# Rewriting the head of an adaLN, selective-scan and mixture-of-experts kernel, and GpSimd's form of the state scaling

## The reference

```
mod = (silu(c) @ wmod).reshape(4, 6, 1, 128)       # sa, ca, ga, sb, cb, gb
h = layernorm(x) * (1 + ca) + sa                   # x: 4 x 1024 x 128
gate = sigmoid(h @ W2 + b2)
u = sigmoid(causal_conv4(h @ W1 + b1) + conv_b)    # 256 channels
xp = u @ x_proj_w                                  # 64 + 16 + 16 columns
delta = softplus(xp[:64] @ dt_proj_w + dt_proj_b)
B, C = xp[64:80], xp[80:96];  A = -exp(A_log)      # 16 states per channel
state[n] = exp(delta * A[n]) * state[n] + delta * B[n] * u
y = sum_n state[n] * C[n] + u * D_skip
x = x + ga * ((y * gate) @ Wo + bo)
h = layernorm(x) * (1 + cb) + sb
x = x + gb * moe(h)                                # 8 experts of 352, the best 2 of each token
```

## Time and profile before

| | |
|---|---|
| median of 3 runs | 698.61 us (697.56 to 700.04) |
| profiled execution, its own time | 697.62 us |
| its span in the profile | 695.8 us |
| PE busy | 615.6 us (88%) |
| DVE busy | 552.0 us (79%) |
| ACT busy | 535.4 us (77%) |
| POOL busy | 517.3 us (74%) |

### The profile page before, as it was taken

One profiled execution on the slowest core, in us unless ns is written; L12 is line 12 of the kernel. 1 busy time (PEld: TensorE's weight loads), 2 busy tenths in 40 slices (PEclk: granted clock), 3 DMA queues, 4 the chain that ended last, 5 costly groups with the idle time before them and its releaser, 6 DMA issues.

```text
span 695.8 us, 14462 instructions
## 1 busy us (share of the span) xinstructions
PE 615.6 (88%) x4435; PEld 512.3 (74%) x4435; DVE 552.0 (79%) x1170; ACT 535.4 (77%) x1000; POOL 517.3 (74%) x453
## 2 busy tenths in 40 slices
PE   3986889989988998997999898769789999999995
PEld 3444757867767675785777677658578999999994
DVE  4347779999989999999999999989986586555554
ACT  3268998997998997999799799797834756566650
POOL 3147969988799899989989999986964647644441
PEclk9999999999999999999999999899999999999998
DMA  7030336434943454534455335466711223222545
GB/s 237 0 123 2 102 86 161 135 93 129 320 122 106 115 129 128 162 101 109 119 148 136 105 100 129 128 182 178 177 30 55 65 62 86 81 69 65 152 145 193
DMA packets 65194, 82.92 MB, mean 119 GB/s; under 512 B 6960, under 2 KB 55152, under 8 KB 61024
## 3 DMA queue, kind: packets, MB, share of 16 engines
q1 hardware_dynamic: 59648, 70.78, 37.2%
q0 software_dynamic: 4320, 9.12, 4.0%
q10 hardware_dynamic: 1152, 2.10, 0.8%
HBM read 52.19 MB, written 29.78 MB: 118 GB/s over the span
## 4 chain that ended last, share of the span: by engine, by line
PE 43%; ACT 36%; DVE 11%; issue 7%; DMA 1%; POOL 1%; DVEq 0%; SPq 0%; ACTq 0%; POOLq 0%
PE psum L589 26%; PE psum L593 16%; ACT S L1006 12%; ACT dA L1014 11%; DVE ring L1370 5%; ACT L953 1%; ACT xn L918 1%; ACT soft L946 1%; ACT soft L945 1%; ACT soft L953 1%; ACT soft L950 1%; ACT L1014 1%; DMA ring<-results 1%; ACT hT L900 1%; ACT psum L958 1%
## 5 line engine op out<-in xcount | busy, mean ns | idle before, releaser
L559 POOL TENSOR_TENSOR ring<-ring,Cb 128x1024 f32<-128x1024 f32 x128 | 279.6, 2186 | 36.7 <-DVE ring L1370 36.2
L593 PEld LDWEIGHTS psum<-ident,S 128*128 128x128 f32 x1024 | 118.6, 143 | 113.5 <-issue 67.7
L593 PE MATMUL psum<-ident,S 128*128 128x128 f32 x1024 | 159.2, 279 | 42.7 <-DVE ring L1370 14.3
L1014 ACT ACTIVATE dA<-delta,A 128x512 f32<-128x512 f32 x256 | 178.6, 716 | 10.3 <-DVE ring L1370 10.1
L1006 ACT ACTIVATE S<-duT,BT 128x256 f32<-128x256 f32 x384 | 166.4, 501 | 24.3 <-DVE duT L1110 20.2
L593 PE MATMUL psum<-ident,ring 128*128 128x128 f32 x1088 | 159.5, 278 | 4.2 <-DMA ring<-results 3.8
L1370 DVE TENSOR_TENSOR_SCAN ring<-dA,state,psum 128x512 f32<-128x512 f32 x128 | 157.6, 1265 | 1.0 <-PE psum L593 0.4
L1370 DVE TENSOR_TENSOR_SCAN ring<-dA,psum 128x512 f32<-128x512 f32 x128 | 150.2, 1206 | 8.8 <-PE psum L593 8.2
L593 PEld LDWEIGHTS psum<-ident,ring 128*128 128x128 f32 x1088 | 129.5, 144 | 5.2 <-DMA ring<-results 4.3
L581 POOL DMA_INDIRECT results<-xn,result_at x71 | 68.7, 968 | 74.6 <-DVE xn L1503 64.9
L589 PE MATMUL psum<-uT,S 128*128 128x128 f32 x852 | 107.2, 275 | 1.0 <-DVE uT L1481 1.0
(11 more groups left out here) (218 smaller groups left out, 734.2 us busy)
## 6 DMA issues: line engine op xcount, KB each, us to landing
Cb<-c_rows SPq DMA_DIRECT2D x32, 1024.0 KB, 6.0
token_rows<-zeros SPq DMA_DIRECT2D x64, 272.0 KB, 7.1
uT<-token_rows SPq DMA_DIRECT2D x71, 68.0 KB, 1.8
ring<-results SPq DMA_DIRECT2D x8, 512.0 KB, 5.0
xT<-in_xT SPq DMA_DIRECT2D x4, 512.0 KB, 4.9
out_T<-xT ACTq DMA_DIRECT2D x8, 256.0 KB, 2.8
stage<-in_xT SPq DMA_DIRECT2D x6, 256.0 KB, 7.7
gateup_w<-in_gate SPq DMA_DIRECT2D x1, 1408.0 KB, 9.5
```

Source lines behind the costliest of these rows:

```text
L559: nc.gpsimd.tensor_tensor(ring[:, k % RING, :, 0:BANK], ring[:, k % RING, :, 1:], Cb[:, group_ % 2, own, :].unsqueeze(1).to_broadcast([P, ...
L593: return nc.tensor.matmul(out, block_in, ident[at, at], is_transpose=True, start=start, stop=True, skip_group_check=True)
L1014: nc.scalar.activation(dA[:, (k * HALVES + a) % DA_SLOTS, :], delta[:, s % 2, a, :], ACT.Exp, scale=A[:, a, n:n + 1]).then_inc(da_ready, 1)
```

## The change

The head (everything ahead of the step loop) is no longer two windows of gaps but a list of its own on each engine.

- Roots: blocks 0 and 1 get theirs from GpSimd too, one `pow` each (`front_root`), VectorE adding epsilon before and multiplying by the mean after (`front_shift`, `front_means`); the Ln, Exp and Newton steps go. Blocks 2 and 3, 4 and 5 follow in the head, 6 and 7 in the first scan segment (GpSimd gap 1, VectorE gap 6). The tail's root has its epsilon added on VectorE in gap 18.
- Folding W1 with the conv weights is done by GpSimd in two halves (`fold`).
- Banks: `home(name, f)` gives the results of blocks 0 and 1 banks of their own (`HEAD_HOMES`), and block 1's h its own tile.
- Orders: see the lists. ScalarE makes both halves of the first softplus in a row with one load of the Ln table; VectorE's part is `first_softplus`, which keeps its intermediate in SBUF (`yg`). TensorE does the first xproj product before the transposes of u. The statistics of the last two blocks stand right ahead of the first scan.
- Idle products: `warm(8)` ahead of the modulation product and `warm(6)` after the first raw transposes, into bank 3, read by nobody.
- One-tensor scaling: GpSimd makes each of its chunks of S with one TENSOR_SCALAR, with BT's column as the per-partition scalar and a second operation times 1.0. `add_bias` gets the second operation as well.
- `minus_half` stands elsewhere in memory, `eps` is gone and `frs` smaller.

```diff
@@ constants @@
 def pool_scaled(k):
-    return sum(pool_chunks(j) > 0 for j in range(k + 1))
+    return sum(pool_chunks(j) for j in range(k + 1))
...
+        HEAD_HOMES = {("xn", 1): "B4", ("u0", 1): "B1", ("u1", 0): "FT", ("u1", 1): "FT", ("uT0", 0): "FT", ("uT1", 0): "B0",
+                      ("gate0", 0): "B0", ("gate1", 0): "B4", ("dt1", 0): "FA", ("dT1", 0): "FA", ("bt", 0): "B1"}
+        def home(name, f):
+            return HEAD_HOMES.get((name, f), "FB" if name in ("xproj", "bt", "dt0", "dt1", "dT0", "dT1") else "FA")
@@ gpsimd @@
+            def front_root(first, last, shifts):
+                part = slice(CS * first, CS * last)
+                pool.wait_ge(fshift_ready, shifts)
+                nc.gpsimd.tensor_tensor(frs[:, 0, part], frs[:, 0, part], minus_half[:, part], ALU.pow).then_inc(froot_ready, 1)
+            def fold(a):
+                at = slice(a * P, (a + 1) * P)
+                nc.gpsimd.tensor_tensor(w1c[:, :, at], w1[:, at].unsqueeze(1).to_broadcast([P, CONVK, P]),
+                                        convb.rearrange("p (d k) -> p k d", k=CONVK)[:, :, at], ALU.mult).then_inc(w1c_ready, 1)
...
-                    nc.gpsimd.tensor_tensor(S[:, k % S_SLOTS, CS - own:, :], duT[:, s % 2, CS - own:, :],
-                                            BT[:, s % 2, CS - own:, n:n + 1].to_broadcast([P, own, MLP]), ALU.mult
-                                            ).then_inc(scaled_pool, 1)
+                    for c in range(CS - own, CS):
+                        nc.gpsimd.tensor_scalar(S[:, k % S_SLOTS, c, :], duT[:, s % 2, c, :], BT[:, s % 2, c, n:n + 1], 1.0,
+                                                ALU.mult, ALU.mult).then_inc(scaled_pool, 1)
+            front_root(0, 1, 1)
+            pool.wait_ge(loaded["attn"], 16 * ATTN_LOADS)
+            fold(0)
+            front_root(1, 2, 2)
+            fold(1)
             pool.wait_ge(mod_step, MOD_STEPS)
-            for window in (-2, -1):
-                for gap in range(GAPS):
-                    gap_work(gap, window)
+            add_bias(0)
+            for b in (1, 2):
+                front_root(b * SEG, (b + 1) * SEG, b + 2)
+                add_bias(b)
+            add_bias(BATCH - 1)
@@ tensor @@
+            def warm(count):
+                for _ in range(count):
+                    product(bank(3)[:, 0:P], mean_w[:, :], mean_w[:, :])
+            pe.wait_ge(mod_step, 1)
+            warm(WARM_FIRST)
...
             for f in range(SEG):
                 raw_turns(f)
+            warm(WARM_SECOND)
+            front(14, 0)
             pe.wait_ge(corr_ready, HALVES)
...
+            pe.wait_ge(w1c_ready, 1)
+            for k in range(CONVK):
+                tap(0, 0, k)
             pe.wait_ge(mod_step, MOD_STEPS)
+            front(14, 1)
+            for f in (SEG, SEG + 1):
+                raw_turns(f)
+            pe.wait_ge(w1c_ready, HALVES)
+            for k in range(CONVK):
+                tap(0, 1, k)
             for a in range(HALVES):
-                product(FT[:, a * P:(a + 1) * P], ones[:, :], Ddiag[:, a, :])
+                pe.wait_ge(read[f"u{a}"], 1)
+                pe.wait_ge(const_ready, XBIAS)
+                last = product(FB[0:PROJ, :], xproj[:, a, :], u[:, 0, a, :], a == 0, a == HALVES - 1)
+            last.then_inc(filled["xproj"], 1)
+            last_read["FB"] = (read["xproj"], 1)
+            for f in (SEG + 2, SEG + 3):
+                raw_turns(f)
+            project(3, 0)
+            last_read["FB"] = (delta_ready, 1)
+            project(6, 0)
+            last_read["FA"] = (delta_ready, HALVES)
+            project(9, 0)
+            front(30, 0)
+            front(1, 0)
...
+            for f in (SEG + 4, SEG + 5):
+                raw_turns(f)
+            front(2, 0)
+            pe.wait_ge(const_ready, CONSTS)
+            for k in range(CONVK):
+                tap(1, 0, k)
+            front(5, 0)
+            project(24, 0)
+            tap(1, 1, 0)
+            project(26, 0)
+            pe.wait_ge(read["u0"], 2)
+            front(30, 1)
+            pe.wait_ge(stat_read, CS * SEGS)
             for a in range(HALVES):
                 turn_in(0, a)
+            tap(1, 1, 1)
+            pe.wait_ge(read["gate1"], 1)
+            for a in range(HALVES):
+                turn_in(1, a)
+                tap(1, 1, 2 + a)
+            front(31, 1)
@@ scalar @@
-            act.wait_ge(mod_step, 2)
-            for step in range(2):
-                front_seeds(step)
+            front(13, 0)
+            act.wait_ge(mod_step, MOD_STEPS)
+            act.wait_ge(zeroed, 2)
+            front(16, 0)
             act.wait_ge(loaded["attn"], 16 * ATTN_LOADS)
             nc.scalar.activation(A[:, :, :], A[:, :, :], ACT.Exp).then_inc(a_exp, 1)
...
+            front(13, 1)
+            act.wait_ge(const_ready, ZHALF)
+            front(22, 0)
+            front(16, 1)
+            front(28, 0)
+            act.wait_ge(const_ready, XBIAS)
+            front(2, 0)
+            for gap in (5, 8, 9, 10):
+                project(gap, 0)
+            for a in range(HALVES):
+                one_more(0, a)
+            bt_copy(0)
+            for a in range(HALVES):
+                nc.scalar.activation(lw[:, a, :], ev[:, a, :], ACT.Ln, bias=1.0).then_inc(lw_ready, 1)
+            front(22, 1)
+            act.wait_ge(const_ready, A_SIGNED)
+            for a in range(HALVES):
+                decay(0, a)
+            scale_in(0)
+            act.wait_ge(const_ready, B2HALF)
+            front(7, 0)
+            scale_in(1)
+            for a in range(HALVES):
+                decay(1, a)
+            front(4, 0)
+            front(28, 1)
@@ vector @@
             for f in range(SEG):
                 raw_stats(f)
+                front_shift(f, f + 1)
+            front_means(0, 1, 1)
...
+            for b in (1, 2):
+                for f in (b * SEG, b * SEG + 1):
+                    raw_stats(f)
+                front_shift(b * SEG, (b + 1) * SEG)
+                if b == 2:
+                    front(31, 0)
+                    front(2, 0)
+                    dve.wait_ge(drow_filled, 1)
+                    V.tensor_copy(Drow[:, :], bank(4)[:, 0:MLP]).then_inc(const_ready, 1)
+                front_means(b * SEG, (b + 1) * SEG, b + 2)
             dve.wait_ge(const_ready, CONSTS)
...
+            first_softplus()
+            for gap in (25, 27):
+                project(gap, 0)
+            for f in (SEGS - 2, SEGS - 1):
+                raw_stats(f)
+            front_shift(SEGS - 2, SEGS)
+            front(31, 1)
```

More of the change, by code:

```diff
@@ L222, in stat_bank @@
         def stat_bank(f):
[L224 to L231, removed]
+            return bank(f if f < SEG else 2 + f % 2)
         PX = bank(6)[:, 0:P]
@@ L718, in gap_work @@
                 call = routed(window)
-                if window == -1 and 14 <= gap < 27:
-                    front_ = None
                 if tail_ is not None:
@@ L757, in start_y, with raw_turns @@
                                          start=(c == c0 and a == 0), stop=True, skip_group_check=True)
+            def warm(count):
+                for _ in range(count):
+                    product(bank(3)[:, 0:P], mean_w[:, :], mean_w[:, :])
+            def raw_turns(f):
+                pe.wait_ge(loaded_x[f // SEG], 16)
+                wait(pe, stat_read, CS * (f - 1) if f >= SEG + 2 else 0)
+                for c in range(CS):
+                    last = turn(stat_bank(f)[:, c * P:(c + 1) * P], xT[:, f * BANK + c * P:f * BANK + (c + 1) * P])
+                last.then_inc(stat_filled, 1)
+            pe.wait_ge(mod_step, 1)
+            warm(WARM_FIRST)
             pe.wait_ge(loaded["c"], 48)
@@ L764, in _ @@
             pe.wait_ge(setup, SETUP)
-            def raw_turns(f):
-                pe.wait_ge(loaded_x[f // SEG], 16)
-                if f == SEG + 2:
-                    pe.wait_ge(mod_step, MOD_STEPS)
-                wait(pe, stat_read, CS * (f - 2) if f >= SEG + 3 else 0)
-                for c in range(CS):
-                    last = turn(stat_bank(f)[:, c * P:(c + 1) * P], xT[:, f * BANK + c * P:f * BANK + (c + 1) * P])
-                last.then_inc(stat_filled, 1)
             for f in range(SEG):
                 raw_turns(f)
+            warm(WARM_SECOND)
+            front(14, 0)
             pe.wait_ge(corr_ready, HALVES)
@@ new lines, in _ @@
+            project(6, 0)
[3 more added lines that the diff above has]
+            front(1, 0)
+            pe.wait_ge(const_ready, D_MADE)
+            pe.wait_ge(read["xn"], 2)
+            for a in range(HALVES):
+                last = product(bank(4)[:, a * P:(a + 1) * P], ones[:, :], Ddiag[:, a, :])
+            last.then_inc(drow_filled, 1)
+            for f in (SEG + 4, SEG + 5):
+                raw_turns(f)
+            front(2, 0)
@@ L937, in project @@
                 if gap == 12:
[L938 to L940 removed]
+                    bt_copy(f)
+                if gap in (12, 21):
```

(5 more changed lines are left out.)

262 lines of the change are left out of this document (117 added, 145 removed).

## The result

The changed kernel takes 694.11 us (693.12 to 695.04, 5 runs) against 698.41 (697.40 to 700.04, 5 runs): ratio 0.994, 95% interval 0.9923 to 0.9958. It gained 4.3 us where 13.7 were forecast, and lies 4.1 us above the end of the range. Its profiled execution has 694.11 us of its own and a span of 692.1, 3.7 less than the span before.

What follows compares the result with a forecast made beforehand. ScalarE was taken to set the pace from the end of the head on, so head savings of 8.65 + 5.0 = 13.65 us come off the end. From 697.6 that left 683.9, for the median 684.9; range 683 to 687.

Steps and rivals of the forecast that it cites:

- Step 1: Head, statistics to first tap: ScalarE starts 3.9 us earlier; first tap at 15.2 us with the clock high.
- Step 2: Head, folded weights moved from VectorE to GpSimd: 1.05 to 2.1 us a half, no effect on the time.
- Step 3: Head, TensorE's clock: with idle products high at the first tap, 2.95 us less for the first passes.
- the first rival: Head: the clock is low at the taps, 10.0 us gained, 688.5 us; chance 0.22.
- Steps 4 to 7: Head, second half of u to ScalarE's loop: 1.3, 6.7 and 0.95 us less, then 2.65 more.
- X: The point in the head where the projection is complete, forecast at 26.0 us, before at 34.67.
- Step 8: Scan phase: shorter GpSimd scaling, the last root and the tail's shift on VectorE change nothing in the time.
- The slower side: Scan phase: GpSimd's single-tensor scaling costs 0.89 us instead of 0.62, giving 707 us; chance 0.04.
- The freed GpSimd time: Scan phase: TensorE gets its scaling sooner, half a microsecond a segment, giving 681 us; chance 0.13.
- The missed-wait rival: Head: the hand-made order has an overlooked wait, 3 to 6 us more, 689.5 us; chance 0.13.

Runs made afterwards that it cites:

- roots_first: shift_back with GpSimd making both early roots ahead of both folds: 686.61 us.
- shift_back: The kernel after with the tail's epsilon added on GpSimd again, as before: 688.46 us.
- scaling_alone: The kernel before with the new one-tensor scaling on GpSimd and nothing else: 696.75 us, ratio 0.9990.
- more_idle_products: roots_first with 12 instead of 6 idle products behind the first raw transposes: 685.31 us.
- scaling_back: The kernel after with GpSimd's scaling again as one product with the broadcast column of BT: 698.96 us.
- shift_alone: The kernel before with the tail's epsilon added by VectorE in gap 18 and nothing else: 707.02 us.
- no_idle_products: roots_first with no idle products at all: 687.01 us.

## Why the prediction failed, step by step

**Step 1, statistics to first tap.** The first tap came at 16.36, not at 15.2. The arithmetic of what was removed holds: the root of GpSimd took 1.05 us from 10.51 (estimate 1.04 from 10.4). Missing is the 1.4 us of the held product, a term that the step doesn't have: "Nothing else is waited for". roots_first, which takes away what held it, has the product in 0.16.

**Step 2, the fold.** 1.53 us a half, between the bounds, there at 13.08 and 15.54 and waited for by no tap. "I take nothing" was still wrong: it looked at who waits for the fold, not at whom the fold holds: VectorE's product with the means lasts 1.49 us beside the first half and 1.48 beside the second, and 0.16 in roots_first beside none.

**Step 3, the clock.** 5.14 us for the first passes, 1.7 over the forecast, whose 2.95 us are the difference of 6.39 and 3.44 in the earlier trace rows, the lengths of the same eight passes that the low and the high clock stand for here; no run shows a frequency. It is not one execution's chance: the five profiles with the head and the idle products of the kernel after have 5.14 to 5.96. The forecast took one unbroken stretch of work to be enough, and named the low clock as the first rival; the kernel fell between, with the low clock for part of the passes (5.14 between 3.44 and 6.39). The table of windows has the granted clock at 0.50 in 16 to 18 us, 0.67 in the next and 1.00 behind it:

```profile
12.00:14.00 2.00, 0.27 (x2) 0.00 (x0) 1.75 (x6) 0.87 (x3) 2.00 (x2) 1.00 1.01 391
...
16.00:18.00 2.00, 1.64 (x2) 0.84 (x3) 1.58 (x7) 1.97 (x4) 0.65 (x1) 0.50 0.04 15
18.00:20.00 2.00, 2.00 (x4) 0.85 (x3) 0.51 (x4) 1.16 (x4) 0.00 (x0) 0.67 0.01 4
20.00:22.00 2.00, 2.00 (x8) 0.93 (x7) 0.00 (x0) 0.09 (x1) 0.00 (x0) 1.00 0.00 0
```

TensorE was busy for 0.27 of the 2 us from 12 to 14, while the transposes waited for the normalised rows, which waited for the held product.

**Steps 4 to 7** held to a few tenths. From the end of the first passes to X: 28.91 - 21.50 = 7.41, 8.68 before: 1.27 less, forecast 1.3. Deltas at X + 10.1 and X + 11.4 (forecast 10.5 and 11.9), first scaling at 42.74 = X + 13.83 (13.85), first scan at X + 16.58 (17.0), ScalarE's step 2 at X + 20.82 (21.0), with the 1.93 us of ScalarE waiting before the second tanh of block 1 that was named. The head is short of the forecast by 13.65 - 10.92 = 2.7 us: 1.16 from step 1, 1.70 from step 3, little else.

**Step 8 failed**, the step with no sum in it: "In the tail a shift of four columns goes from GpSimd (0.19) to VectorE: nothing." It costs 5.2 us by shift_back, in the profiles 1.0 us a segment (58.95 against 57.95). Its price was taken from the row of the same instruction on the other engine, and VectorE was thought to have slack for 0.2 us a segment. It has hardly any for 1.5: it is busy 55.15 of 59 us, and the scans behind it feed everyone. GpSimd's wait for the scans over 172 to 404 us was 11.1 us; between the third and the sixth load of Ln it is 7.0 before, 14.8 after and 10.7 in shift_back. The other terms of step 8 held: scaling 0.48 us (taken 0.40, bounds 0.40 and 0.89), the last root 1.64 (1.7), and no segment time from a shorter scaling beyond the 1 us of scaling_alone.

Of the 10.0 us by which the span misses the sum (13.65 forecast, 3.7 measured), the head has 2.7, the scans 5.7 and the experts 1.5.

**The rivals.** The slower side, a scaling of 0.89 us, did not come. The freed GpSimd time is the 1.2 us above, not 3. The missed-wait rival put the fault in the order of the roots in the head and came to 689.5; the waits were as planned, and no semaphore is at fault. A held engine has no releaser in the profile: it shows as a busy row that is too long, as the 1.82 us at 249.38, which names none.

**What stays open.** The experts took 1.5 us more of the span. In the nine profiles with the new head that stage has 185.0 to 187.0 us, in the three with the old one 183.0 to 184.6. In seven of the nine the last gather of results stands in the chain with 7.3 to 7.9 us; with the old head it has 5.8 to 6.0. The piece of the kernel after:

```profile
679.59 7.27 DMA ring<-results
```

The nine also share the other placement in memory (`minus_half`, `eps`, `frs`), so that is as good a suspect as the head; neither was tried alone, nor a further run of the old head.

The best version is more_idle_products, 685.31 us and 0.9818 (0.9781 to 0.9855), but roots_first and its other variants are not told apart from it; all of them beat both kernels. That they come near the forecast of 684.9 is in part luck: in all of them GpSimd's fold still holds the second product with the means, the experts take 1.5 us or more longer than before, and the first passes are at the high clock in some and not in others.

## What to carry to other kernels

Price an instruction that changes engines by its neighbours there: in this kernel a TENSOR_SCALAR of four columns from SBUF to SBUF on VectorE lasted, in six of its eight times, until the end of what GpSimd was running, up to 2.54 us in the kernel after and 2.8 in scaling_back and shift_alone; a column at a time it took 0.32 for the four, on GpSimd itself 0.2. In a profile look for rows whose mean is far above their minimum and which end together with a row of GpSimd (here a mean of 1.46 us and a minimum of 0.16): no wait and no releaser is shown for the row at 249.38. When one edit looks good beside another, run the square of both before crediting either: here the new scaling was worth 4.5 us beside the fault and 1.2 without it.

## What the runs showed that was not expected

*Which forms are held.* By GpSimd's products of two tensors: TENSOR_SCALAR with one source of four columns (up to 2.54 us), and instructions with two SBUF inputs, even of one column (1.09 us in the kernel before, 1.48 to 1.58 in the kernel after). By its one-tensor instructions with two operations too: the two-input row at 15.67 above (0.99 us), and a TENSOR_SCALAR of two columns that in roots_first ended with GpSimd's add_bias (14.72, 1.12 us):

```profile
14.87 1.00 DVE L1526 TENSOR_SCALAR zhalf<-zhalf 128x2 f32<-128x2 f32 x1
```

Not held: one source and one column (0.144 us), and the RECIPROCAL (0.18 us). Beside the add_bias of the kernel before, which has one operation and ran from 12.33 to 15.27, VectorE's instructions with two SBUF inputs took 0.17 us (14.76 and 14.96); beside that of the kernel after the product with the means took 0.17 at 27.06, begun 0.05 us behind it, and was held at 34.23 (0.42 us). Nor did GpSimd's power hold one-source instructions that started in it, from 13.04 to 14.05 in the kernel after:

```profile
13.29 0.25 DVE L1517 TENSOR_SCALAR xproj<-xproj 128x192 f32<-128x192 f32 x1
...
13.60 0.16 DVE L1519 TENSOR_SCALAR gaquarter<-mod 128x4 f32<-128x4 f32 x1
```

Why these differ is open; each was seen only where this kernel happens to put it.

*The fold's pattern* on GpSimd costs 1.53 us for 512 elements, against 1.05 for the scaling product of 512 in the earlier trace rows.

*The clock at the start isn't the program's alone.* Up to the modulation the kernel after and roots_first issue the same work to TensorE, the eight idle products with it. The same twelve products of the modulation took, in the one and in the other:

```profile
5.21 2.69 PE L596 MATMUL psum<-siluc,ring 128*128 128x4 f32 x12 [0.31 <-ACT siluc L1071]
```

```profile
5.28 1.47 PE L598 MATMUL psum<-siluc,ring 128*128 128x4 f32 x12 [0.45 <-ACT siluc L1073]
```

So a forecast of the level at a given microsecond of the head has an uncertainty, here 1.2 us for twelve products, that the eight idle products don't take away. The column of the granted clock doesn't help there: it reads 1.00 over 16 to 22 us of no_idle_products, while the eight passes take 5.93 us, near the 6.39 of the low clock. The window and TensorE's timeline:

```profile
16.00:22.00 6.00, 6.00 (x13) 2.45 (x12) 2.00 (x8) 2.45 (x7) 0.98 (x1) 1.00 0.02 6
```

```profile
15.48 5.93 PE L598 MATMUL psum<-hT,w1c 128*128 128x512 f32 x8
```

In the kernel before the column reads 1.00 too from 20 to 26 us, in the passes that took 6.39 us:

```profile
20.00:26.00 6.00, 6.00 (x9) 2.14 (x8) 0.00 (x0) 0.00 (x0) 0.00 (x0) 1.00 0.00 0
```

In both stretches the lengths of the matmuls tell the clock, and the column doesn't.
